# A decoder layer on one core: self-attention in place, batches in pairs on half arrays, feed-forward as a pipeline

## The reference

```python
q = transpose(x, (2, 0, 1))                       # self-attention: per position l, over the 32 batches
prob = softmax(einsum('lnc,lmc->lnm', q, q) / sqrt(64))
x = layernorm(x + (x + transpose(einsum('lnm,lmc->lnc', prob, q))))

qh = softmax(Wq x, over the 64 of a head) / 8      # cross-attention: per batch, 8 heads of 64
kh = softmax(Wk ctx, over the 512 positions); vh = Wv ctx
out = Wo (kh vh^T)^T qh + bo                       # then L2-normalized over channels, times g * 8
x = layernorm(x + out)

g, u = mx_linear(x, w_gate), mx_linear(x, w_up)    # 512 -> 1376
x = layernorm(x + mx_linear(silu(g) * u, w_down))  # 1376 -> 512
```

## Time and profile before

| | |
|---|---|
| three runs | 1016.91, 1008.45, 1012.99 us |
| profiled execution, span | 1010.8 us (the profile gives no other time for it; first to last instruction) |
| busy PE / PEld / DVE / ACT / POOL | 809.3 / 545.3 / 759.0 / 568.5 / 437.1 us |
| mean granted PE clock | 0.894 |
| DMA | 38.77 MB in 30372 packets, 25.92 MB read from HBM |
| instructions | 17612, of them 5463 matmul records |

### The profile page before, as it was taken

How to read it: one execution, slowest core, us unless ns; L and a number is a source line. 1 busy time by engine, 2 the same in 40 slices (tenths; PEclk the granted TensorE clock), 3 DMA queues, 4 the chain that set the end, 5 groups by cost and what they waited for, 6 DMA issues and landing times.

```text
span 1010.8 us, 17612 instructions
## 1 busy us (share of the span) xinstructions
PE 809.3 (80%) x5463; PEld 545.3 (54%) x5463; DVE 759.0 (75%) x1660; ACT 568.5 (56%) x1051; POOL 437.1 (43%) x491
## 2 busy tenths in 40 slices
PE   2115555548999999999999999999999867778873
PEld 2104555524767676676766667676667633333331
DVE  3766777748788888888888888888888266666663
ACT  1119777636666666766666676666667223333332
POOL 4423333313445455454545545454553334444443
PEclk7557676659999999999999999999999789999997
DMA  8993111101001101101100110110010000000000
GB/s 201 204 200 137 32 31 31 37 21 32 14 19 31 22 9 31 31 1 30 31 21 10 31 31 0 31 31 21 10 31 1 1 1 30 23 21 21 21 21 31
DMA packets 30372, 38.77 MB, mean 38 GB/s; under 512 B 4496, under 2 KB 16784, under 8 KB 30352
## 3 DMA queue, kind: packets, MB, share of 16 engines
q1 hardware_dynamic: 30352, 38.51, 15.9%
HBM read 25.92 MB, written 4.19 MB: 30 GB/s over the span
## 4 chain that ended last, share of the span: by engine, by line
PE 58%; issue 14%; POOL 8%; DMA 8%; DVE 6%; ACT 5%; SPq 1%; POOLq 0%; ACTq 0%; DVEq 0%
PE bank L1247 11%; PE bank L1204 11%; PE bank L1240 11%; PE bank L1223 5%; PE bank L1170 5%; PE bank L1211 5%; ACT big L873 4%; PE bank L1234 4%; DMA big<-in_ctx_dram 4%; POOL big L545 3%; POOL rstd L540 3%; DMA big<-in_L_ffn_w_down_dram 2%; PE bank L1301 2%; DMA big<-in_L_ffn_w_up_dram 2%; DVE big L565 1%
## 5 line engine op out<-in xcount | busy, mean ns | idle before, releaser
L873 ACT ACTIVATE big<-bank 128x512 f32<-128x512 f32 (+4 forms) x368 | 195.3, 588 | 53.1 <-PE bank L1223 31.5
L475 POOL TENSOR_TENSOR big<-big 128x512 f32<-128x512 f32 x128 | 131.5, 1057 | 81.1 <-DVE big L722 81.1
L1204 PE MATMUL bank<-big,WkT 128*128 128x512 f32 x256 | 136.2, 614 | 13.0 <-DMA big<-in_ctx_dram 8.8
L873 ACT ACTIVATE big<-big 32x256 f32<-32x256 f32 (+6 forms) x160 | 120.3, 772 | 15.6 <-DVE big L766 9.9
L963 ACT ACTIVATE big<-big,q_scales 128x512 f32<-128x512 f32 x128 | 92.4, 722 | 64.3 <-DVE big L712 64.3
L960 ACT ACTIVATE big<-bank,big 128x512 f32<-128x512 f32 x128 | 87.7, 685 | 68.6 <-DVE big L705 67.5
L1247 PEld LDWEIGHTS bank<-big 128*128 128x128 f32 x1024 | 120.6, 194 | 5.6 <-DVE big L742 1.2
L1247 PE MATMUL bank<-big 128*128 128x64 f32 x1024 | 119.4, 275 | 1.0 <-DVE big L742 1.0
L1240 PE MATMUL bank<-big 128*128 128x512 f32 x256 | 116.7, 598 | 0.5 <-ACT big L873 0.5
L718 DVE TENSOR_REDUCE big<-big 128x8 f32<-128x512 f32 x128 | 87.1, 680 | 25.7 <-ACT big L963 24.7
L705 DVE TENSOR_REDUCE big<-bank 128x1 f32<-128x512 f32 x128 | 88.2, 689 | 17.5 <-PE bank L1204 14.4
(11 more groups left out here) (116 smaller groups left out, 1406.1 us busy)
## 6 DMA issues: line engine op xcount, KB each, us to landing
big<-big SPq DMA_DIRECT2D x64, 128.0 KB, 2.3
big<-in_x_dram SPq DMA_DIRECT2D x2, 2048.0 KB, 17.3
big<-in_x_dram SPq DMA_DIRECT2D x4, 1024.0 KB, 11.2
xt<-in_x_dram SPq DMA_DIRECT2D x1, 4096.0 KB, 15.0
big<-in_ctx_dram SPq DMA_DIRECT2D x16, 256.0 KB, 2.7
out_dram<-big SPq DMA_DIRECT2D x16, 256.0 KB, 2.0
big<-in_L_ffn_w_down_dram SPq DMA_DIRECT2D x4, 688.0 KB, 6.7
big<-in_L_ffn_w_gate_dram SPq DMA_DIRECT2D x10, 256.0 KB, 2.7
```

The source lines that it names most:

```text
L475: pool.tensor_tensor(e, e, r, ALU.mult).then_inc(s.p_ready, 1)
L873: return act.activation(dst, src, ACT.Copy)
L1204: pe.matmul(bank[i % 2][:], WkT[:, par, P * i:P * i + P], ctxs, start=True, stop=True).then_inc(s.klog_ready, 1)
```

## The change

The whole program is rewritten; the arithmetic blocks stay.

- Order of loads: one row of w_down and two rows of gate and up weights, then x once in token layout in four pieces, the projections, xq in four pieces, then the rest. xsw, x with its row halves swapped, is made on chip (swap_down on DVE, swap_up on ACT).
- Self-attention: chunks of 16 positions (CL = 16), three score buffers. Scores take weights and moving side straight from x in token layout, at a stride of one position row, on both row halves. Messages take xq at its own stride as weights, in two column halves. DVE's add_msg covers 128 rows at once. copy_x and copy_q are gone; spread_probs masks the blocks with a scale of 0 or 1.
- Cross-attention goes by tile (two batches). Key and query logits are pairs of K=64 matmuls on the two row halves, both fp32; the fp16 split and the x1 round trip are gone. A products are pairs with M=64; y is computed transposed, as pairs with M=64 and N=512; square sums and the spreading of norms are small matmuls. Query maxima, shifts and exponentials cover both batches at once; POOL adds the halves of each head (fold_p) before DVE sums. Layer norm is applied by ACT, y is added by POOL. Sixteen weight items are rounded one a tile.
- Feed-forward: four hidden buffers, two each of hq, hqT, yo and xo; PSUM banks for gate, up and down alternate.
- The order on every engine is written out (first_groups, slot_groups, middle_groups, turn_groups, last_groups and the call lists), as Python loops without Fori, so all waits are on constants.

```diff
-    CL = 8
+    CL = 16
...
+            def scores(c):
...
+                        last = pe.matmul(bank[c % 2][B * j:B * j + B, B * l:B * l + B], both_x[rows, :, at],
+                                         x_by_batch[j // 2][:, :, :, at], start=True, stop=True)
...
+            def messages(c, h):
...
+                    for par in range(2):
+                        p = pd[:, c % 2, CL // 2 * h + l, :, T * par:T * par + T].rearrange("p j t -> p t j")
+                        last = pe.matmul(o[C * par:C * par + C, C * l:C * l + C], xq[:, :, CL * c + CL // 2 * h + l], p,
...
+            def k_logits(f, i):
...
+                for par in range(2):
+                    rows = slice(C * par, C * par + C)
+                    pe.matmul(bank[par][:], WkT[rows, P * i:P * i + P], ctxs[rows, f % 2],
+                              start=True, stop=True).then_inc(s.klog_ready, 1)
+
+            def q_logits(f, i):
...
+                    pe.matmul(bank[2 + par][:], xt[rows, f, P * i:P * i + P], WqT[rows, :],
+                              start=True, stop=True).then_inc(s.qlog_ready, 1)
...
+            def a_product(t, i):
...
+                    last = pe.matmul(bank[6][rows, :], ctxT[:, i, rows], ET[:, par, i % 2],
+                                     start=(i == 0), stop=(i == NT - 1))
...
+            def y_product(t, j):
...
+                    last = pe.matmul(bank[7][C * par:C * par + C, :], GTs[:, par, j], PTs[:, par, j],
+                                     start=(j == 0), stop=(j == NJ - 1))
...
+            def fold_p(f, i):
...
+                pool.tensor_tensor(qfold[:, i % 2], e[:, :, :, 0:DH // 2], e[:, :, :, DH // 2:DH], ALU.add
+                                   ).then_inc(s.q_folded, 1)
...
+            def dequant_aw(a):
...
+                pool.tensor_tensor(groups(awbf[:, a % 2, 0:n]), groups(aw8[:, 0:n]),
+                                  spread(aw_scale[:, a % 3, 0:n // GRP], n // GRP), ALU.mult).then_inc(s.aw_quantized, 1)
...
+            for f in range(5, T - 3):
+                k_logits(f, 0)
+                transpose_p(f - 2, 1, 2)
+                transpose_k(f - 1, 0, 1)
+                q_logits(f, 0)
+                transpose_p(f - 2, 0, 3)
+                y_product(f - 2, 0)
+                transpose_p(f - 2, 1, 3)
+                transpose_k(f - 1, 1, 0)
+                y_product(f - 2, 1)
...
```

More of the change, by code:

```diff
@@ new lines, in decoder_kernel @@
+        for t, group in first_groups:
+            tr_no[t, group] = len(tr_no)
+        for f in range(5, T - 3):
+            for behind, group in slot_groups:
+                if f - behind in tiles:
+                    tr_no[f - behind, group] = len(tr_no)
+        for t, group in middle_groups:
+            tr_no[t, group] = len(tr_no)
+        for u in range(7, 9):
+            for behind, group in turn_groups:
+                if u - behind in tiles:
+                    tr_no[u - behind, group] = len(tr_no)
@@ L333, in decoder_kernel, with aw_group @@
+        for t, group in last_groups:
+            tr_no[t, group] = len(tr_no)
+        def aw_group(a):
+            return (a, "d1") if a < DN else (a - DN, "gu")
+        aw_last = tr_no[aw_group(AW - 1)]
         block = stack.enter_context(nc.Block())
@@ new lines, in _ @@
+            silu(6, 0)
+            copy_h(3, 1)
+            result(0)
+            silu(6, 1)
+            copy_xT(7)
+            silu(6, 2)
+            silu(7, 0)
+            copy_h(4, 0)
+            result(1)
+            copy_h(4, 1)
+            silu(7, 1)
+            copy_xT(8)
+            result(2)
+            for u in range(9, T - 6):
+                copy_h(u - 4, 0)
+                silu(u - 2, 2)
+                silu(u - 1, 0)
+                copy_h(u - 4, 1)
+                result(u - 6)
+                silu(u - 1, 1)
+                copy_xT(u)
@@ new lines, in _ @@
+            copy_h(6, 0)
+            silu(8, 2)
+            silu(9, 0)
+            copy_h(6, 1)
+            copy_xT(T - 6)
+            silu(9, 1)
+            result(4)
+            copy_h(7, 0)
+            silu(9, 2)
+            silu(T - 6, 0)
+            copy_h(7, 1)
+            result(5)
+            silu(T - 6, 1)
+            silu(T - 6, 2)
+            copy_xT(T - 5)
+            copy_h(8, 0)
+            copy_xT(T - 4)
+            silu(T - 5, 0)
+            copy_h(8, 1)
+            silu(T - 5, 1)
@@ new lines, in _ @@
+            result(6)
+            silu(T - 5, 2)
+            silu(T - 4, 0)
+            copy_h(9, 0)
+            silu(T - 4, 1)
+            copy_h(9, 1)
+            result(7)
+            silu(T - 4, 2)
+            copy_xT(T - 3)
+            result(8)
+            silu(T - 3, 0)
+            silu(T - 3, 1)
+            copy_xT(T - 2)
+            silu(T - 3, 2)
+            silu(T - 2, 0)
+            copy_h(T - 6, 0)
+            copy_h(T - 6, 1)
+            result(9)
+            copy_xT(T - 1)
@@ new lines, in g_product @@
+            def g_product(t):
+                pe.wait_ge(s.at_copied, t + 1)
+                if t:
+                    pe.wait_ge(s.y_normed, t)
+                for j in range(NJ):
+                    for h in range(2):
+                        for par in range(2):
+                            rows, cols = slice(C * par, C * par + C), slice(C * h, C * h + C)
+                            last = pe.matmul(bank[7 - par][cols, C * j:C * j + C],
+                                             ATs[rows, P * j + C * h:P * j + C * h + C], Bs[rows, j, cols],
+                                             start=True, stop=True)
+                            if j == NJ - 1 and h == 1:
+                                last.then_inc(s.gt_ready, 1)
@@ new lines, in down @@
+            def down(u, r):
+                pe.wait_ge(s.tr_copied, tr_no[u, f"h{r}"] + 1)
+                if r == 0:
+                    if u == 0:
+                        pe.wait_ge(s.gt_copied, 2 * T)
+                    elif u == 1:
+                        pe.wait_ge(s.y_normed, T)
+                    else:
+                        pe.wait_ge(s.down_added, u - 1)
+                f0, f1 = ((0, 6), (6, FT))[r]
+                for f in range(f0, f1):
+                    m = P if f < FT - 1 else FR
+                    last = pe.matmul(bank[6 + u % 2], hqT[0:m, u % 2, f], wdT[0:m, f], start=(f == 0), stop=(f == FT - 1))
+                last.then_inc(s.down_part, 1)
@@ new lines, in _ @@
+            scores(0)
+            project(0)
+            project(1)
+            scores(1)
+            scores(2)
+            scores(3)
+            scores(4)
+            project_wo()
+            scores(5)
+            project_b()
+            scores(6)
+            scores(7)
+            messages(0, 0)
+            messages(0, 1)
+            messages(1, 0)
+            transpose_down(0, 0)
+            messages(1, 1)
+            k_logits(0, 0)
+            messages(2, 0)
+            messages(2, 1)
```

3565 lines of the change are left out of this document (2573 added, 992 removed), and 10 rows, old and new, of the table first_groups.

## The result

The changed kernel takes **731.32 us** (median of 4 runs, 731.22 to 732.56); the kernel before took 1010.84 beside it (1008.45 to 1016.91). The ratio is 0.7229, with a 95% interval of 0.7199 to 0.7260. The forecast was 751, in a range of 700 to 800.

The account below looks back on a forecast made before the run. Each stage had its own limit: transfers, a wait chain at half clock, PE in cross-attention, one chain in feed-forward. 1010.8 - 116 - 95 - 51 = 749 us of span, median 2 above: 751 us, range 700 to 800.

Parts of the forecast that it names:

- A: Loading and self-attention, up to the first query logits: 107 us forecast for 222.9 before, a change of -116 us.
- B: Cross-attention, first query logits to first gate product: 30.5 us a tile, 483 us in all, a change of -95 us.
- C: Feed-forward, first gate product to the end: 8.6 us a tile, 158 us in all, a change of -51 us.
- Messages can begin at about 48: Self-attention: messages start once xq, loaded behind the projections, has landed, at about 48 us (45 to 67).
- the stride factor: Self-attention messages: reading xq at a 512-byte stride costs 1.7 times, 48 us instead of 28, taken from an ACT copy.
- Rival 3: Self-attention: strided fp32 reads cost three times, messages 84 us, first query logits at 168, total 812 us; chance 0.10.
- 40.0 a tile in series: Cross-attention: PE's time per tile if neighbouring matmuls do not run at once; 24.3 us if they do.
- Rival 2: Cross-attention: K=64 row pairs run in series, PE 34.3 us and period 35.7 a tile, total 834 us; chance 0.12.
- for a near tie I take 90%: Cross-attention: PE and DVE both near 27.5 us a tile reach only 90% busy, giving 30.5 us a tile.
- the forecast's 5: Cross-attention: 5 us taken off the 488 for all tiles because the keys of tile 0 are done early.
- Rivals 1 and 4: First: everything packs, DVE bounds B at 27.5, 703 us, chance 0.17. Second: engines interlock, tile near 35, 823 us, 0.04.
- rival 5: Cross-attention: packed matmuls run in series and each shape change drains for long, so the kernel gets slower; chance 0.03.

Follow-up runs that it names:

- e1: The changed kernel with the scores' weights and moving side read from 32 neighbouring columns of x instead of strided elements: 723.89 us.
- e2: The changed kernel with the messages' weights read from 64 neighbouring columns of xq instead of elements 512 bytes apart: 722.77 us.
- e12: The changed kernel with x loaded first, ahead of the first weights row and two weight items: 730.13 us.
- e13: The changed kernel with scores read from neighbouring columns and only 8 of 64 channels of xq loaded: 711.41 us.
- e3: The changed kernel with only 8 of the 64 channels of xq loaded, the rest set to zero by POOL before: 724.38 us.
- e4: The changed kernel with the key logits as full-row K=128 matmuls with zero-padded weights instead of K=64 row pairs: 768.61 us.
- e11: The changed kernel with PE's list in the loop over tiles 5 to 12 regrouped to 23 shape changes a tile instead of 30: 725.42 us.
- e6: The changed kernel with the query maximum taken over 16 of each head's 64 columns, relieving VectorE: 727.64 us.
- e5: The changed kernel with two of four pairs of y products per tile multiplying only 64 of 512 columns, relieving PE: 712.41 us.
- e7: The changed kernel with the hidden tile's rescaling moved behind the next clip in ten places of VectorE's feed-forward list: 733.11 us.
- e8: The kernel before with its loops written out on every engine, work and order the same: 1004.12 us.
- e9: The changed kernel with PE's list in the loop over tiles 5 to 12 regrouped to 21 shape changes a tile instead of 30: 749.12 us.

## Why the forecast held, point by point

**The total is 20 us off, and two errors of opposite sign stand behind it**: A came 15 us later and B 35 us sooner than forecast, C within 1. That A took back 15 of B's 35 is luck; with either error alone the time would still have been inside 700 to 800 (716 without A's, 766 without B's).

**Part A, mechanism right, two terms off.** Scores started at 21.0 (forecast 22). "Messages can begin at about 48" failed: 70.5. The terms: the scores' own records, taken at 17 us, took 31, since the stride factor that I gave to the messages holds for the scores too (30 ns against 15, e1); I had covered them by the wait for xq. Above that, PE's 13.5 us of unnamed idle time stood in no term. It is PE waiting for its own instructions: the gaps stand 256 instructions apart in the list, inside chunks that wait for nothing, and in five kernels (the one after, e1, e2, e12, e13) all nineteen of over 0.7 us end 1.3 to 1.8 us after a packet of 16384 bytes of instructions lands. e3 shows that in the kernel after they hang on the xq transfer. The Trainium skill (Runtime: NRT & Kernel Launch, Instruction fetch mechanics) says that a sequencer fetches its program itself over a DMA queue, in blocks of 256 instructions. The trace agrees: 16384 bytes a packet, and gaps 128 matmul records and their 128 weight loads apart. The page calls the cost at the end of a block mostly hidden: in attention it is (PE busy 298.6 of 300 us), beside the strided scores and the transfer of xq it was 13.5 us. From the first message to the first query logits it took 51.8 us, not 59: the stride factor is 1.3 (e2), not 1.7. Rival 3, each side slower and messages from 73, was near on where the messages begin, in part for another reason, and wrong on what they cost: 77 ns a record is 2.5 us for 32 of them, where it had 5.3.

The neighbours' operations that last until PE's strided chunk ends (0.69 to 3.83 us, gone in e1) stood in no step of the forecast. The Trainium skill (SBUF — State Buffer, Who interferes with whom) says that PE and ACT never wait on anyone; here ScalarE's exponential took 3.80 us instead of 0.63, so the measurement decides.

**Part B, overlap as taken, the 90% wrong.** Row pairs overlap: 0.96 to 1.06 against the forecast's 0.9 to 1.0, and without it e4 takes 37 us more. (The forecast's 40.0 a tile in series is not the sum of its own terms, which is 38.3; nothing measured hangs on it.) Rival 2 falls. Shape changes: 30 a tile at 0.15 (e11, and the distances in one tile) are 4.5 us in place of 3. With 4.5 the forecast's terms would give 28.8; the period is 28.34, so the rest of the sum came some 0.5 lower than its 24.3. The failed step is "for a near tie I take 90%": PE was busy 298.6 of 300 us. VectorE, at 25.2 us a tile (267.03/300 of the period) and not 27.5, had 3 us of slack; e6 shows that nothing hung on it, e5 that everything hung on PE. 28.34 x 16, less the forecast's 5, is 448, and 447.8 was measured. Rivals 1 and 4 fall with that, rival 5 too.

**Part C, 159 against 158, but not for all the reasons given.** The gate products of tile 0 start at 570.1 and those of tile 15 at 697.4, 8.5 us a tile, where 8.6 was taken. (The 11.35 us that the forecast gives for the kernel before is the distance of one pair of tiles; by the same measure, 801.7 to 981.3, its mean was 12.0.) The contention of VectorE with POOL is there (3.77 us once, mean 1.79), and e7 shows that removing it gains nothing. And the writing out of the loops alone gave the kernel before 6.5 us in this part (e8), a term that the prediction lacked, beside the 50 us gained. What sets 8.5 us is open: VectorE 48 of 50, PE 46, with ScalarE's activation and POOL's scales in one chain between them.

**The load order** was in the sum as the start of the scores. e12 shows it to be worth nothing that the intervals can tell.

## What to carry to other kernels

Where one engine has most of the work and its order is written out with slack for the others, take its busy time as the period, not busy time over an efficiency (here 28.2 of 28.34 us); then count its changes of shape. Price a strided operand on every matmul that reads it, those that seem hidden included, and look at what the other engines do beside it. Where a list is written out and its instructions are short, look for idle time that no engine ends and that stands at even distances in the list, and compare it with when the trace's packets of instructions land. Before moving an instruction in a list, ask which later entry of a neighbour's list stands behind the copy that follows from it: one such wait of 2.2 us a tile took back all that nine changes fewer gave and 13 us more, and where the clock fell behind it another 1.7 us a tile.

## What the runs showed that was not expected

- fp32 matmuls with both operands strided (64x32, one 4-byte element from each position) take 30 ns a record, against 15 contiguous, at granted clock 0.50 and 1.00 alike; and most VectorE, ScalarE and POOL operations that overlap them last until about their end (0.69 to 3.83, 0.63 to 3.80; POOL's 1376-column shift 2.51 in e1, 7.25 in the kernel after), but VectorE's maximum of the scores does not (0.69).
- PE, with 256 instructions in 3.9 us or less, stood still for its own program: 2.3 to 8.4 us at a time while bulk transfers filled the DMA, and 0.7 to 4.2 us when they did not (e13), each time until 1.3 to 1.8 us after the next 16384 bytes of instructions had landed.
- A change of shape between row or column pairs and the full array costs 0.14 to 0.16 us by the distances within a tile, and 0.15 by e11.
- Zero-padded K=128 pairs take 1.81 us where packed K=64 pairs take 1.06.
- Of eight equal idle times of 2.2 us, PE kept its full granted clock behind five, and the clock fell behind three (0.57 on the mean of 408 to 412; e9).
